# MLP layer 1 of a fused image kernel: from eight matmuls on split, stacked inputs to four 32-row tiles, and the ELU on two PSUM banks per instruction

## What is computed

```python
x = x + conv3x3_mixed_of_3_experts(_gn(x))   # softmax routing on the pooled image
x = x + depthwise3x3(abs(_gn(x)))
x = x + box_mean_17x17(_gn(x))
x = x + mlp(_gn(x))

# mlp(v):
nbr = sum of the 8 neighbours of v, zero padded
xn  = jnp.repeat(nbr, 8, axis=1)             # 16 channels -> 128
h = elu(einsum('bchw,oc->bohw', xn, w1))     # 128 -> 64
h = elu(w2 h); h = elu(w3 h); h = elu(w4 h)  # 64 -> 64, three times
F = w5 h                                     # 64 -> 64, then means of 4 groups * 0.1 -> 16
```

## Time and profile before

| what | value |
|---|---|
| three runs | 957.66, 961.74 and 1212.97 us |
| median | 961.74 us |
| profiled execution, first to last instruction (its span) | 960.3 us |
| PE busy in it | 827.8 us, 86% |
| DVE busy | 760.5 us, 79% |
| ACT busy | 628.2 us, 65% |
| POOL busy | 227.6 us, 24% |

### The profile page before, as it was taken

The page is one execution under the profiler, slowest core; times in us unless marked ns, Lnnn a source line. Parts: engine busy times, 40 slices in busy tenths (PEclk is TensorE's granted clock), DMA queues, the critical chain, the costliest instruction groups (busy, mean ns, idle before and its releaser), DMA issues.

```text
span 960.3 us, 9306 instructions
## 1 busy us (share of the span) xinstructions
PE 827.8 (86%) x2391; PEld 397.9 (41%) x2391; DVE 760.5 (79%) x1267; ACT 628.2 (65%) x1105; POOL 227.6 (24%) x296
## 2 busy tenths in 40 slices
PE   2759786688999899998999899989998998979993
PEld 1423443353444345443445344444444452424330
DVE  2645674767989888988888898989897689878994
ACT  1020213476877768696878787787878687978883
POOL 2030143111512115122412151213312122221000
PEclk9979887988999999999999999999999899999997
DMA  5425423414020320214020402032112002001201
GB/s 97 77 43 93 86 37 71 88 23 74 8 61 16 59 38 17 60 24 72 16 60 16 67 13 62 15 58 38 34 44 47 17 17 61 16 16 41 54 16 44
DMA packets 68751, 43.18 MB, mean 45 GB/s; under 512 B 5602, under 2 KB 62306, under 8 KB 68722
## 3 DMA queue, kind: packets, MB, share of 16 engines
q1 hardware_dynamic: 66976, 42.57, 23.0%
q10 hardware_dynamic: 1746, 0.27, 0.2%
HBM read 9.67 MB, written 8.39 MB: 19 GB/s over the span
## 4 chain that ended last, share of the span: by engine, by line
PE 34%; DVE 28%; ACT 13%; DMA 10%; issue 6%; SPq 5%; POOL 2%; DVEq 0%; ACTq 0%; POOLq 0%
PE pz L700 17%; DVE g L908 8%; PE pc L644 6%; DMA xs<-in_x_dram 5%; ACT u L577 5%; ACT u L586 5%; DMA halo<-y 4%; DVE bn L828 4%; SPq L395 3%; DVE box_sum L961 3%; DVE u L903 3%; PE pc L659 3%; DVE box_sum L946 2%; ACT u L583 2%; PE pc L672 2%
## 5 line engine op out<-in xcount | busy, mean ns | idle before, releaser
L700 PE MATMUL pz<-g,wT 128*128 128x512 f32 x768 | 362.6, 611 | 11.7 <-DVE g L908 9.6
L577 ACT ACTIVATE u<-pz,s_row 128x512 f32<-128x512 f32 x354 | 241.6, 686 | 123.2 <-PE pz L700 121.9
L908 DVE SCALAR_TENSOR_TENSOR g<-pz,k_row,u 128x512 f32<-128x512 f32 x348 | 247.4, 744 | 57.2 <-ACT u L586 55.7
L586 ACT ACTIVATE u<-u 128x512 f32<-128x512 f32 x472 | 286.5, 635 | 1.3
L700 PEld LDWEIGHTS pz<-g,wT 128*128 128x128 f32 x768 | 144.9, 194 | 203.2 <-issue 113.2
L828 DVE BATCH_NORM_STATS2 bn<-xs 128x6 f32 (+1 forms) x128 | 87.1, 688 | 29.7 <-DMA xs<-in_x_dram 19.8
L696 PE MATMUL pz<-stack,w1T 128*128 128x512 f32 x256 | 83.8, 448 | 20.2 <-DMA stack<-near_rest 12.8
L659 PE MATMUL pc<-y,t 128*128 128x512 f32 x192 | 93.5, 625 | 5.2 <-DVE t L365 5.2
L669 PE MATMUL pc<-y,t 128*128 128x512 f32 x192 | 92.7, 620 | 2.4 <-ACT y L551 2.4
L577 ACT ACTIVATE u<-pz 128x512 f32<-128x512 f32 x118 | 68.2, 602 | 39.8 <-PE pz L696 39.8
L908 DVE SCALAR_TENSOR_TENSOR g<-pz,u 128x512 f32<-128x512 f32 x128 | 81.9, 683 | 11.3 <-ACT u L586 10.3
(11 more groups left out here) (118 smaller groups left out, 785.2 us busy)
## 6 DMA issues: line engine op xcount, KB each, us to landing
halo<-y SPq DMA_DIRECT2D x96, 120.0 KB, 3.3
xs<-in_x_dram SPq DMA_DIRECT2D x8, 1024.0 KB
stack<-near_rest SPq DMA_DIRECT2D x64, 128.0 KB, 2.3
out_dram<-xs SPq DMA_DIRECT2D x8, 1024.0 KB
stack<-stack SPq DMA_DIRECT2D x32, 128.0 KB, 2.2
halo<-y SPq DMA_DIRECT2D x48, 8.0 KB, 2.6
g<-in_con_late_dram SPq DMA_DIRECT2D x1, 712.5 KB, 9.6
con<-in_con_early_dram SPq DMA_DIRECT2D x1, 272.5 KB, 14.7
```

The lines of the kernel that those rows point to most:

```text
L577: act.activation(u[:, m, :], pz[:, m, :], ACT.Relu, scale=-1.0, bias=s_row[:, l - 1:l] if l else 0.0).then_inc(relu_done, 1)
L586: act.activation(u[:, m, :], u[:, m, :], ACT.Exp, scale=-1.0).then_inc(exp_done, 1)
L700: pe.matmul(pz[:, m, :], wT[:, l - 1, :], g[:, m, :], start=True, stop=True).then_inc(z_mm, 1)
L908: dve.scalar_tensor_tensor(out=elus(j, q, l)[:, m, :], in0=pz[:, m, :], scalar=k_row[:, l - 1:l] if l else 1.0, in1=u[:, m, :], op0=ALU.ad ...
```

## The change

Layer 1 is now four F32 matmuls (`first_layer`), each with the 32 partitions of `near` that hold two pixel rows as its contraction, against 32 rows of `wT[:, 0]`. POOL's split, the `stack` tiles and the three DMAs per chunk are gone, and so is the F32R pair `w1T`. `relu`, `exp` and `join` work on pairs of banks, 128 x 1024 elements in one instruction (h = 0 is banks 0 and 1, h = 1 banks 2 and 3), and PE waits for pairs. The special course for the last images (`clips`, `carried`) is gone. The last layer's result goes to a tile of its own (`g_last`), DVE runs the joins of l = 0 before `output`, and box and near share one pair of tiles (`band_part`).

```diff
-        near_rest = sb("near_rest", [P, CH], F32R)
-        stack = [sb(f"stack{n}", [P, CH], F32R) for n in range(2)]
+        g_last = sb("g_last", [P, M, CH])
...
-            def split_near(j, q):
-
-                if q > 0:
-                    pool.wait_ge(z_mm, zn(j, q - 1, 0, M - 1))
-                elif not (isinstance(j, int) and j == 0):
-                    pool.wait_ge(z_mm, zn(j - 1, Q - 1, 0, M - 1))
-                pool.wait_ge(conv_evac[3], Q * j + q + 1)
...
             def elu(j, q, l):
 
-                def relu(m):
-                    act.wait_ge(z_mm, zn(j, q, l, m))
-                    act.activation(u[:, m, :], pz[:, m, :], ACT.Relu, scale=-1.0,
+                for h in range(2):
+                    pair = slice(2 * h, 2 * h + 2)
+                    act.wait_ge(z_mm, zn(j, q, l, h))
+                    act.activation(u[:, pair, :], pz[:, pair, :], ACT.Relu, scale=-1.0,
                                    bias=s_row[:, l - 1:l] if l else 0.0).then_inc(relu_done, 1)
...
-                    relu(0)
-                    for m in range(1, M):
-                        relu(m)
-                        exp(m - 1)
-                    exp(M - 1)
+                    act.wait_ge(relu_done, zn(j, q, l, h))
+                    act.activation(u[:, pair, :], u[:, pair, :], ACT.Exp, scale=-1.0).then_inc(exp_done, 1)
...
+            def first_layer(j, q):
+
+                if q > 0:
+                    pe.wait_ge(g_written, zn(j, q - 1, LAYERS - 1, 1))
+                elif not (isinstance(j, int) and j == 0):
+                    pe.wait_ge(g_written, zn(j - 1, Q - 1, LAYERS - 1, 1))
+                pe.wait_ge(conv_evac[3], Q * j + q + 1)
+                for m in range(M):
+                    rows = slice(32 * m, 32 * m + 32)
+                    last = pe.matmul(pz[:, m, :], wT[rows, 0, :], near[rows, q * CH:(q + 1) * CH], start=True, stop=True)
+                    if m % 2:
+                        last.then_inc(z_mm, 1)
+
+            def hidden_layer(j, q, l):
+
+                for h in range(2):
+                    pe.wait_ge(g_written, zn(j, q, l - 1, h))
+                    for m in (2 * h, 2 * h + 1):
+                        last = pe.matmul(pz[:, m, :], wT[:, l, :], g[:, m, :], start=True, stop=True)
+                    last.then_inc(z_mm, 1)
...
-                        for n in range(2):
-                            last = pe.matmul(pz[:, m, :], w1T[n][:, m, :], stack[m // 2][:, :], start=n == 0, stop=n == 1)
-                        last.then_inc(z_mm, 1)
...
+            def joins(j, q, l):
+
+                for h in range(2):
+                    dve.wait_ge(exp_done, zn(j, q, l, h))
+                    pair = slice(2 * h, 2 * h + 2)
+                    dve.scalar_tensor_tensor(out=elus(l)[:, pair, :], in0=pz[:, pair, :], scalar=k_row[:, l - 1:l] if l else 1.0,
+                                             in1=u[:, pair, :], op0=ALU.add, op1=ALU.max).then_inc(g_written, 1)
...
-                            if last and not apart(*last):
-                                output(*last)
-                            elu(t - 1, p, l)
-                            if last and apart(*last):
-                                output(*last)
+                            joins(t - 1, p, l)
+                            if l == 0 and part_before(t, p):
+                                output(*part_before(t, p))
```

180 lines of the change are left out of this document (37 added, 143 removed).

## The result

The changed kernel takes **1027.22 us** (median of four runs, 1020.38 to 1030.51) against 962.32 us for the one before. One of the four executions of the kernel before took 1212.97 us, and the ratio leaves it out: it is **1.068**, with a 95% interval of 1.063 to 1.074. The forecast was 1004 us, 972 to 1034. So the direction and the range held, and the loss is 65 us where 42 were forecast. The profiled execution took 1028.82 us, with a span of 1027.0.

The account below looks back on a forecast made before the run. The prediction took the matmul, relu, exp, join ring as the bound, with no engine having much room. 960.3 + 24 (full rounds) + 10 (round 7) + 21 (round 8) + 3 (clock) - 16 (start) = 1002.3, median 1004 us, range 972 to 1034.

Parts of the forecast that it names:

- the ring: Hidden layers on pairs: matmul, relu, exp, join to the next layer's matmul takes 5.48 us for half 0 (5.4 to 5.7).
- the start: Setup and round 1: PE's waits for DMAs behind the loads of x go, and setup shrinks, -16 us in all.
- 4.5 together: Start: the 2.73 us wait goes, with part of the 3.78 us of a layer 1 at low clock: 4.5 us saved.
- 1.5, an estimate: Setup: two DVE instructions of 512 columns, eight small copies and three transposes less save 1.5 us.
- rival of serial tiles: Layer 1: row tiles run one after another, taking 3.4 us, so the kernel takes 1029 us; chance 0.15.
- Sum: 4.0 a round: Full rounds: losses of 0.2, 0.85, 0.4, 0.3, 1.5 and 0.8 us add to 4.0 a round, +24 over 6 rounds.
- expert l = 3 to box l = 1 ... 0: Full rounds: this stretch, 13.5 us before, is set by DVE's scan and statistics and does not change.
- Four chunks of 23.1: Round 8: four chunks at 4.5 + 5.5 + 5.5 + 7.6 = 23.1 us each give 92.4 us against 70.9, +21.
- +3** (0 to 15 ...): Low clock after PE rests of 3 us at chunk ends in round 8: +3 us, 0 to 15 if whole layers are slow.
- about 3 more: Round 7: about 3 us beyond the four rings' 92.3, where y3, the sums and their copies delay joins; round +10.
- Nothing is lost in full rounds: Rival: pairs cost little more than single banks, the ring closes in 4.8 us, 967 us, no change; chance 0.14.
- Faster: Rival: the ring closes and ACT's work sets the tail, about 17 us a chunk, so 934 us; chance 0.09.

Follow-up runs that it names:

- loads later: Kernel before, with the loads of images 6 and 7 moved in SP's queue behind round 1's stacking DMAs: 951.33 us, 0.987.
- tiles only: Kernel before with only the new layer 1 in four tiles, each waiting for its own bank; single banks, `clips` and `carried` stay: 972.55 us, 1.008.
- more work for PE: Changed kernel with added matmuls in round 8 whose result nothing uses, one behind each of l = 0 to 2, three behind l = 3: 1023.38 us, 1.061.

## Why the prediction was right, and where its sizes were off

**Right: the ring.** The mechanism is shown from four sides. With pairs the loss is there without any tile (1.079 with the old layer 1), single banks with the new layer 1 have hardly any of it (1.007, with the 10 us of round 1 gained), shortening the ring by 0.43 us takes 13 us away, and the steps in the trace are the sum of its four parts. What the small rearrangements that come with the pairs cost was not timed alone. The price of a join over two banks, for which no row stood, was well placed between its bounds.

**Right: the start.** -10 us for round 1's wait; the round's difference of -6.5 is that less the ring's +4, and "loads later" shows the wait by itself (-12 us, 0.987). The setup terms were off: "4.5 together" and "1.5, an estimate" gave 6 us ahead of the first layer 1, and 1.7 came. The old layer 1 started at 154.76, the tiles start at 153.11: the wait of 2.73 us is gone, but the neighbour sums ahead of it came later themselves (their last matmuls start at 150.25 instead of 149.09). A difference of 1.7 is also less than profiles differ: with the old layer 1 on single banks the first one starts at 154.8 to 161.1 in four traces (two of them with loads moved).

**Right: tiles side by side.** 1.14 us for eight records when all four wait once, and no gap to the next mode at 535.51. The rival of serial tiles fell. The Trainium skill's "TensorEngine Tiling (Array Packing)", section "Key Properties", says that a change of mode drains the engine. The trace shows no gap between the records, but not that the change is free either. L612's weight loads start only with its first matmuls, while those of the tiles' second passes start 0.4 us ahead of them. L612 starts 0.52 us after the last tile's second pass; the second passes of the tiles start 0.53 us after their first, those of L612 0.45. So a change can cost 0.1 us here, and not the 0.2 from which the prediction made 6 us. And where tiles wait one by one they do follow one another (3.02 us in "tiles only"), so that rival was wrong only for this form.

**Mis-sized: the full rounds**, "Sum: 4.0 a round". Averaged over rounds 2 to 6, by the prediction's own parts:

| part | before | after | difference | forecast |
|---|---|---|---|---|
| near l = 3 to expert l = 1 | 12.10 | 13.36 | +1.26 | +0.8 |
| expert l = 1 to 3 | 13.74 | 13.74 | 0 | 0 |
| expert l = 3 to box l = 1 | 13.40 | 13.79 | +0.39 | 0 |
| box l = 1 to 3 | 10.05 | 11.42 | +1.37 | +0.85 |
| box l = 3 to depthwise l = 1 | 16.80 | 16.73 | -0.1 | +0.4 |
| depthwise l = 1 to 3 | 14.79 | 15.37 | +0.58 | +0.2 |
| depthwise l = 3 to near l = 1 | 12.99 | 13.66 | +0.67 | +0.3 |
| near l = 1 to 3 | 9.77 | 11.27 | +1.50 | +1.5 |
| sum | 103.6 | 109.3 | +5.7 | +4.0 |

The kinds and places were right, five of eight terms too small. The ring itself is 5.60 and not 5.48, because the pair is ready after 2.02 us instead of "0.86 more, 1.91". The likely reason is that PE now stands still before a pair, and its first weight load starts only with it (584.16 in the rows above). That is 0.1 in each of four steps. Box has one step of 7.13 at the low clock in one of the five rounds (0.3 on average). The depthwise step behind the join on which y3 and the neighbour sums wait is 7.33 instead of 6.87, where 0.2 was given. And "expert l = 3 to box l = 1 ... 0" assumed that DVE's statistics end when they did: they end 11.93 us after the start of l = 3 instead of 11.54, since the joins of l = 3 end 0.2 us later there and the scan behind them takes 1.76 us instead of 1.59.

**Mis-sized: rounds 7 and 8 and the clock.** "Four chunks of 23.1" is 92.4; the ring alone gives 93.9, as round 8 of "more work for PE" shows, so this is right to 1.5 us. The rest, 5.9 us, is the low clock in round 8, where "**+3** (0 to 15 ...)" was given for the clock as a whole. In round 7 the box part takes 23.9 us and the near part 25.1, near the forecast; the depthwise part without a convolution takes 29.5 instead of 23.1, and the expert part 24.8. In the depthwise part stand steps of 7.36, 7.32 and 10.26 us where the ring alone gives 5.60, 5.60 and 7.69. The middle one has its records at full clock (4.07 us): it ends with a wait of 3.25 us for a join, which DVE began at 877.25 after four us of making y and box sums. The other two have records of 5.46 and 6.65 us, at the low clock in part or nearly whole. They cost 1.8 and 2.6 us, and DVE's work 1.7, which the "about 3 more" had foreseen.

In sum, the spans differ by 66.7 us where the terms gave 42. Of the 24.7 that were missing, 4.3 lie ahead of the first layer 1, 8.5 in the full rounds, 7.9 in round 7 and 4.9 in round 8, with 0.9 the other way in the rest. No single term carries the miss; the one most under its size is the clock's. It counted rests of 3 us before single matmuls at the ends of chunks in round 8. It left out that every layer of round 8 now has a rest of 1.5 to 1.9 us, that layers in the two parts of round 7 without a convolution have rests of up to 3.3 us, and that layers would run at the low level behind them: 5.9 us in round 8 and some 5 in round 7.

In total the clock's mean fell from 0.952 to 0.937, 37 us more at 1.2 GHz. How much of that belongs to the tiles and how much to the pairs is only hinted at by two traces: pairs with the old layer 1 have 0.945 (113 us at the low level, 30 of them in rounds 7 and 8), the changed kernel 0.937 (129 us, 51 in rounds 7 and 8).

**The rivals.** "Nothing is lost in full rounds" needed a ring of 4.8 and fell with the 5.60. "Faster" fell with it. What spoke for it did come true, less work for ACT and DVE: ACT's busy time fell by 17 us, DVE's by 68, and it bought nothing.

## What to carry to other kernels

Where a few engines pass the same data round in a ring, count first how many pieces are in flight and how long one piece takes around; merging instructions makes busy shares fall and the ring longer. Here a layer of the box and near parts went from 4.8 to 5.6 us and one of the last round from 4.2 to 5.6, and the ring decides once no engine is full. Undoing the merge of the one step that can start on its first half (relu) gave back 13 us, and exp and join on pairs still left 1.052; so a price per instruction is no reason to merge any step of such a ring. And if a change has two halves, time each alone: here the half that removed a wait of 10 us had its gain hidden under the loss of the other, and the wait could be taken out by moving two loads in a queue.
